# Dividing attended rows instead of probabilities, and two changes to when side work waits, in a stacked cross-attention kernel

## Chip, cores and metric

The kernel runs on 1 core of one Trainium2 chip. The metric is the device time of one execution in microseconds (us), lower is better; the median of several runs is what is compared. The engines are TensorE (PE; its weight loads are listed as PEld), VectorE (DVE), ScalarE (ACT), GpSimd (POOL) and SyncE (SP), which issues the DMAs.

## What is computed

Four attention blocks are applied to x (32 batches of 56 tokens, 160 features) with a context of 1500 keys of 96 features per batch. The parts that matter here:

```python
x = L0(x, ctx)   # three small attentions over 16 keys each, 8 heads; 0.5, 0.5 and 1.0 as weights
x = L1(x, ctx)   # self-attention over 56 tokens (20 heads), cross-attention over 1500 keys, feed-forward
x = L2(x, ctx)   # cross-attention over 1496 keys (8 heads), plus
                 #   ca_hs1 = _mha(ca_q1, residual, residual); ca_hs2 = _mha(ca_hs1 @ Wq, ca @ Wk_ca, ca @ Wv_ca)
x = L3(x, ctx)   # self-attention over 56 tokens (20 heads of 8), cross-attention over 1500 keys, feed-forward

def _attend(q, k, v, scale):
    probs = softmax(q @ k.T * scale)      # exp(s - max) / sum
    return probs @ v
```

## The kernel before, in words

**Phases and pairs.** L0 and L1 form phase 0, L2 is phase 1, L3 is phase 2. In each phase the 32 batches are worked off as 16 pairs; each batch has 64 slots of the 128 partitions. Of the 16 pairs the first and the last are written out, and the 14 between are one hardware loop (`Fori(1, PAIRS - 1)`), so a phase has 13 back edges on every engine.

**Main work.** For each half b of a pair (b = 0, 1) `main` runs over 12 chunks of 125 keys times the groups of heads (3 groups, of 8, 8 and 4 heads, in phases 0 and 2; 1 group in phase 1). For each, TensorE makes scores (L1099 to L1101, three matmuls), ScalarE takes the exponential twice (L1768, L1770), GpSimd forms the low part p_lo (L1557), and two groups later TensorE makes the outputs (L1114 to L1116). Scores and outputs are one step each: a half-pair has 72 steps in phases 0 and 2 and 24 in phase 1. The first scores wait for `mr_ready`, the row maxima written into q_hi (L1417).

**Side work.** Everything else is generators that yield a number before each piece: `pre` (layer norms and the small attentions of the next pair), `queries`, `split`, `context` (transposing the long context in 3 pieces of 500 keys: TensorE L1024, ScalarE ctxT_hi L1726, VectorE ctxT_lo L1391, GpSimd ctx_lo L1538), `maxima` (row maxima over the keys: per tile of queries 3 matmuls L1041, each reduced by VectorE at L1407 or L1404; at the end mneg L1412, its matmul L1046 and q_hi L1417), `post` (projection and feed-forward), `normalise` (the division of the long attention's output, through DRAM). The table `PARTS` gives each part its length in numbers and a weight. `lane` lays parts one behind the other over the steps of a half-pair and scales them to fill it, and `weave` emits each side piece when its position comes due, in the same order on every engine. The second half (b = 1) carries the second part of the next pair's `pre`, then its `queries`, `context` and `maxima`; its lane ends with the half-pair, so the last thing ahead of the next pair's first scores is that pair's q_hi. The first half carries the other batch's `split`, `context` and `maxima`, and `post` and the beginning of `pre`.

**The banks.** Side work uses the PSUM tensor ps_c, whose banks are taken in turn: 3 in phases 0 and 2, and 2 in phase 1 (`banks`). Piece r of the context lies in bank r modulo that number. The first maxima matmul waits for `ctl_ready`, the count of context pieces whose low part VectorE has formed, to have reached all three; then matmul n writes bank n modulo the number of banks.

**The small attentions.** `softmax` on VectorE: maximum (L1188), subtraction (L1190), then ScalarE's exponential (L1594), the sum (L1194), its reciprocal (L1196), and the multiplication of all probabilities by it (L1203), which signals `p_ready`. TensorE's `probs_T` (L732) waits for that, transposes the probabilities; ScalarE copies them out (L1684 in phase 2), `out_slots` (L741) multiplies them with the values (40 matmuls of 16 columns in phase 2), VectorE copies the attended rows out into oz (L1353 in phase 2; L1307 and L1327 in phase 1), `out_T` (L750) transposes them and `project` (L758, L666) projects them. Phase 0 has two such attentions per pair, phase 1 two (the second over 4 keys per head, `p2`), and phase 2 one (10 tiles of 128 columns).

Of the kernel before, what the change touches and what calls it, by code (L numbers as in the profile page):

```python
# [69 lines left out]
class At:  # L70
# [27 lines left out]
    "s_psum": ((2, 2, 1), 0), "s_max": ((2, 2, 1), 0), "s_sub": ((2, 2, 1), 0), "s_exp": ((2, 2, 1), 0),  # L98
    "s_sum": ((2, 2, 1), 0), "s_rec": ((3, 2, 1), 0), "p_ready": ((2, 2, 1), 0),
    "pt_psum": ((2, 2, 1), 0), "pt_ready": ((2, 2, 1), 0), "o_psum": ((2, 2, 1), 0), "o_ready": ((2, 2, 1), 0),  # L100
# [31 lines left out]
def xattn_stack(nc, a, sel, hmask, hmask32, out):  # L132

    es = ExitStack()
    with es:
# [265 lines left out]

        POST = 16

        def schedule(eng, side, main):
# [43 lines left out]

            def lane(parts, start=0.0):

                slots = 2 * NC * len(groups(HEADS[now["ph"]])) - start
                total = sum(length for _, _, length, _ in parts)
# [20 lines left out]
            def apart(steps):  # L473

                return steps, []
# [20 lines left out]
            def pair(t, first=False, last=False):  # L496
# [10 lines left out]
                else:  # L507
                    weave(main(t, 0, first=first), lane(parts + end), *norm)
                parts, start = [], 0.0
                if not last:  # L510
                    parts = [pre_b] + before(t + 1, 0)
                elif t.ph < 2:
                    parts, start = [part("pre", side.pre, At(t.ph + 1, 0, ahead=True))], POST + 4.0
                weave(main(t, 1, last=last), lane(parts, start), apart(side.normalise(t, 0)))

# [144 lines left out]
        def _(pe):  # L660
# [8 lines left out]
            class side(Idle):  # L669
# [57 lines left out]
                @staticmethod  # L727
                def probs_T(t, n, tiles, bank):

                    pe.wait_ge(*got("p_ready", t, n + 1))  # L730
                    for k in range(tiles):
                        z = tr(side_banks(t)(0, 128, bank, 128 * k, 128), sm[:, 128 * k:128 * k + 128], ident[:, :])  # L732
                    z.then_inc(*sig("pt_psum"))
# [150 lines left out]
                def pre_1(t):  # L884
# [55 lines left out]
                    yield 22  # L940
                    pe.wait_ge(*got("p_ready", t, 2))
                    tr(side_banks(t)(0, 32, 0, 0, 128), p2[:, :], ident[:, :]).then_inc(*sig("pt_psum"))
# [85 lines left out]
                def maxima(t, b):  # L1028

                    tiles, wide = MAX_TILES[t.ph]  # L1030
                    for k in range(tiles):
                        for r in range(NPIECE):
                            n = NPIECE * k + r
                            yield 1 + n
                            if n == 0:
                                pe.wait_ge(*got("ctl_ready", t, NPIECE * (b + 1)))
                                if b:
                                    pe.wait_ge(*got("ql_ready", t, per("ql_ready", t)))
                            if n >= banks(t):
# [94 lines left out]
        def _(dve):  # L1134
            V = nc.vector

            class side(Idle):
# [47 lines left out]
                def softmax(t, n, src, dst, m, s, axes, half=None):  # L1185
# [10 lines left out]
                    V.reciprocal(s, s).then_inc(*sig("s_rec"))  # L1196
                    k = n + 1 if t.ph else 2 * n + 1
                    dve.wait_ge(*got("s_rec", t, k))
                    if half is not None:
# [4 lines left out]
                        .then_inc(*sig("p_ready"))  # L1204
                    yield

                @staticmethod
# [74 lines left out]
                def pre_1(t):  # L1282
# [22 lines left out]
                    yield 13  # L1305
                    dve.wait_ge(*got("o_psum", t, 1))
                    V.tensor_copy(oz[:, :], side_banks(t)(0, 128, 1, 0, D)).then_inc(*sig("o_ready"))  # L1307
                    yield 17
# [16 lines left out]
                    yield 25  # L1325
                    dve.wait_ge(*got("o_psum", t, 2))
                    V.tensor_copy(oz[:, :], side_banks(t)(0, 128, 1, 0, D)).then_inc(*sig("o_ready"))  # L1327
                    yield 29
# [3 lines left out]
                def pre_2(t):  # L1332
# [18 lines left out]
                    yield 14  # L1351
                    dve.wait_ge(*got("o_psum", t, 1))
                    V.tensor_copy(oz[:, :], C(0, 128, 0, 0, D)).then_inc(*sig("o_ready"))  # L1353
                    yield 18
# [464 lines left out]
```

## Time and profile before

| what | us |
|---|---|
| median of 3 runs | 6804.21 (6771.78 to 6814.81) |
| the profiled execution | 6784.65 |
| its span, first to last instruction | 6782.8 |
| busy in the span: TensorE / its weight loads | 5972.3 / 4873.4 |
| busy: ScalarE / GpSimd / VectorE | 3112.4 / 3018.5 / 2860.2 |

Phase 0 lasts to about 2990 us of the span, phase 1 to about 4210 us, phase 2 to the end; both boundaries hold a prologue in which the weights are folded. TensorE's granted clock over the span is 0.914 of full speed. In the rows below, `<-` behind an idle time names what ended it; "issue" is time in which the engine waited for nothing that the profile shows. In a waits row stand the total, the count and the longest. A timeline row begins with start and duration; `xN` means N instructions merged.

### The profile page before, as it was taken

How to read it: one execution, taken by the hardware profiler on the slowest of the kernel's cores; microseconds unless marked ns; L12 is line 12 of the kernel's file. 1: busy time of each engine (PE TensorE's matmuls, PEld its weight loads, DVE VectorE, ACT ScalarE, POOL GpSimd, SP SyncE). 2: the span in 40 equal slices, each digit the busy share in tenths (PEclk: the TensorE clock that was granted, in tenths of full speed). 3: DMA queues.
4: the chain of work that ended last, by engine and by line, in shares of the span. 5: the costliest groups of instructions: out<-in, count | busy, mean ns of one | idle time of the engine just before them, and what ended most of it. 6: DMA issues, size and time to landing. Idle time of an engine off the chain costs nothing.

```text
span 6782.8 us, 106855 instructions
## 1 busy us (share of the span) xinstructions
PE 5972.3 (88%) x34384; PEld 4873.4 (72%) x34384; DVE 2860.2 (42%) x5026; ACT 3112.4 (46%) x7280; POOL 3018.5 (45%) x2992
## 2 busy tenths in 40 slices
PE   7999998989989999989898988988888888888888
PEld 5777777777777777766666665777777777777776
DVE  1444444444444444424545443544444444444442
ACT  1444444444444444534444442544454444444444
POOL 0344444444444444434545441544444444444545
PEclk8899999999999999979999896999998989989988
DMA  2000000000000000000101011000000000000000
GB/s 50 12 13 14 14 14 14 14 14 14 14 14 14 12 14 14 18 14 22 29 21 29 21 25 24 17 14 14 14 14 14 14 14 17 14 14 14 17 15 9
DMA packets 84450, 114.90 MB, mean 17 GB/s; under 512 B 42814, under 2 KB 64682, under 8 KB 83978
## 3 DMA queue, kind: packets, MB, share of 16 engines
q1 hardware_dynamic: 83978, 108.56, 5.8%
q8 instruction: 302, 4.95, 0.3%
q14 instruction: 170, 1.39, 0.1%
HBM read 104.06 MB, written 4.46 MB: 16 GB/s over the span
## 4 chain that ended last, share of the span: by engine, by line
PE 67%; issue 10%; DVE 9%; ACT 7%; POOL 4%; DMA 2%; ACTq 0%; DVEq 0%; POOLq 0%; SPq 0%
PE ps_c L666 13%; PE ps_c L1041 7%; PE ps_u L1114 6%; PE ps_s L1099 6%; PE ps_s L1100 5%; PE ps_s L1101 5%; PE ps_u L1115 5%; PE ps_u L1116 5%; POOL p_lo L1557 3%; PE ps_c L1060 3%; ACT p_hi L1770 2%; PE ps_c L732 1%; PE ps_c L1081 1%; PE ps_c L844 1%; PE ps_c L741 1%
## 5 line engine op out<-in xcount | busy, mean ns | idle before, releaser
L1557 POOL TENSOR_TENSOR p_lo<-p,p_hi 125x448 fp32r<-125x448 f32 (+2 forms) x2688 | 2708.2, 1018 | 2957.6 <-ACT p_hi L1770 2755.9
L1768 ACT ACTIVATE p<-ps_s 125x448 f32<-125x448 f32 (+2 forms) x2688 | 1323.3, 492 | 2502.2 <-PE ps_s L1101 2286.4
L1407 DVE TENSOR_REDUCE mpiece<-ps_c 125x1 f32<-125x500 f32 (+1 forms) x1984 | 1287.2, 674 | 339.8 <-PE ps_c L1041 320.6
L1770 ACT ACTIVATE p_hi<-ps_s 125x448 fp32r<-125x448 f32 (+2 forms) x2688 | 1313.7, 489 | 0.0
L1099 PE MATMUL ps_s<-q_hi,ctxT_hi 105*125 105x448 f32 (+3 forms) x2688 | 1029.0, 383 | 181.2 <-issue 86.5
L1114 PE MATMUL ps_u<-p_hi,ctx_hi 125*97 125x448 f32 (+2 forms) x2688 | 1026.8, 382 | 85.3 <-POOL p_lo L1557 78.9
L1041 PE MATMUL ps_c<-ctxT_hi,q_hi 96*125 96x500 f32 (+1 forms) x2112 | 874.9, 425 | 131.9 <-DVE ctxT_lo L1391 87.8
L1100 PE MATMUL ps_s<-q_lo,ctxT_hi 96*125 96x448 f32 (+2 forms) x2688 | 961.5, 358 | 0.0
L1101 PE MATMUL ps_s<-q_hi,ctxT_lo 96*125 96x448 f32 (+2 forms) x2688 | 956.8, 356 | 0.0
L1115 PE MATMUL ps_u<-p_hi,ctx_lo 125*96 125x448 f32 (+2 forms) x2688 | 950.8, 354 | 0.0
L1116 PE MATMUL ps_u<-p_lo,ctx_hi 125*97 125x448 f32 (+2 forms) x2688 | 949.6, 353 | 0.0
L1099 PEld LDWEIGHTS ps_s<-q_hi,ctxT_hi 105*125 105x125 f32 (+2 forms) x2688 | 534.9, 199 | 287.6 <-issue 151.6
L1114 PEld LDWEIGHTS ps_u<-p_hi,ctx_hi 125*97 125x97 f32 (+1 forms) x2688 | 465.5, 173 | 233.6 <-POOL p_lo L1557 137.9
L1041 PEld LDWEIGHTS ps_c<-ctxT_hi,q_hi 96*125 96x125 f32 (+1 forms) x2112 | 403.2, 193 | 276.0 <-DVE mpiece L1407 94.5
L1100 PEld LDWEIGHTS ps_s<-q_lo,ctxT_hi 96*125 96x125 f32 (+1 forms) x2688 | 540.7, 201 | 55.5
L1101 PEld LDWEIGHTS ps_s<-q_hi,ctxT_lo 96*125 96x125 f32 (+1 forms) x2688 | 539.2, 201 | 41.0
L1115 PEld LDWEIGHTS ps_u<-p_hi,ctx_lo 125*96 125x96 f32 (+1 forms) x2688 | 467.3, 174 | 96.1
L1116 PEld LDWEIGHTS ps_u<-p_lo,ctx_hi 125*97 125x97 f32 (+1 forms) x2688 | 464.0, 173 | 90.1
L666 PE MATMUL ps_c<-hT,w_m 80*96 80x128 f32 x3072 | 376.0, 283 | 20.6 <-ACT hT L1587 19.4
L666 PEld LDWEIGHTS ps_c<-hT,w_m 80*96 80x96 f32 x3072 | 361.9, 170 | 35.5 <-issue 29.8
L1538 POOL TENSOR_TENSOR ctx_lo<-ctx_raw,ctx_hi 125x1152 fp32r<-125x1152 f32 x96 | 238.9, 2488 | 317.3 <-DVE ctx_hi L1385 317.3
L1365 DVE TENSOR_TENSOR q_lo<-ps_c,q_hi 96x224 fp32r<-96x224 f32 x192 | 74.3, 387 | 444.1 <-ACT q_hi L1705 444.1
(234 smaller groups left out, 6097.4 us busy)
## 6 DMA issues: line engine op xcount, KB each, us to landing
ctx_raw<-in_ctx SPq DMA_DIRECT2D x96, 562.5 KB
pT<-recs SPq DMA_DIRECT2D x32, 420.0 KB, 3.3
w_area<-recs SPq DMA_DIRECT2D x32, 420.0 KB, 3.3
w_area<-recs SPq DMA_DIRECT2D x32, 168.0 KB, 3.5
cs<-in_ctx SPq DMA_DIRECT2D x192, 6.0 KB, 2.7
x_between<-x_out SPq DMA_DIRECT2D x32, 80.0 KB
x_in<-x_between SPq DMA_DIRECT2D x32, 80.0 KB
w_area<-in_L_xattn_wq SPq DMA_DIRECT2D x2, 800.0 KB, 5.7
```

The lines of the kernel that those rows point to most:

```text
L666: z = mm(dst, lhsT(i), rhs(i), start=(first and i == 0), stop=(last and i == 1))
L1041: mm(C(0, wide, n % banks(t), 0, PIECE), q_hi[0:DC, b, wide * k:wide * k + wide], ctxT_hi[0:DC, b, PIECE * r:PIECE * r + PIECE], start=Tru ...
L1099: mm(dst, ctxT_hi[0:rows_, b, k], q_hi[0:rows_, b, q], start=True, stop=False)
L1100: mm(dst, ctxT_hi[0:DC, b, k], q_lo[:, b, q], start=False, stop=False)
L1101: mm(dst, ctxT_lo[:, b, k], q_hi[0:DC, b, q], start=False, stop=True).then_inc(*sig("sc_psum"))
L1114: mm(dst, ctx_hi[0:kp, cb, c, :], p_hi[0:kp, s, 0:w], start=(c == 0), stop=False)
L1115: mm(ps_u[0:DC, g, 0:w], ctx_lo[0:kp, cb, c, :], p_hi[0:kp, s, 0:w], start=False, stop=False)
L1116: mm(dst, ctx_hi[0:kp, cb, c, :], p_lo[0:kp, s, 0:w], start=False, stop=(c == NC - 1)).then_inc(*sig("pv_done"))
L1407: z = V.tensor_reduce(mpiece[0:wide, k, r:r + 1], C(0, wide, n % banks(t), 0, PIECE), AX.X, ALU.max)
L1557: P.tensor_tensor(p_lo[0:kp, k % 3, 0:w], p32[0:kp, k % 2, 0:w], p_hi[0:kp, k % 3, 0:w].bitcast(F32), ALU.subtract).then_inc(*sig("pl_ready"))
L1768: A(p32[0:kp, k % 2, 0:w], ps_s[0:kp, k % 2, 0:w], ACT.Exp, scale=DH[t.ph] ** -0.5)
L1770: A(p_hi[0:kp, k % 3, 0:w], ps_s[0:kp, k % 2, 0:w], ACT.Exp, scale=DH[t.ph] ** -0.5)\
```

## The change

In phases 1 and 2 the small attentions no longer multiply the probabilities by the reciprocal of their sum. TensorE transposes the bare exponentials (it waits for `s_exp`), and VectorE multiplies the attended rows by the reciprocals while it takes them out of PSUM (`weigh`, in place of the copy into oz). Phase 0 keeps its multiplication. The first matmuls of the maxima wait only for the context piece that their own bank held, or that they read. And the side lane of a pair's second half is scaled to end three steps before the half-pair does.

```diff
-    "s_sum": ((2, 2, 1), 0), "s_rec": ((3, 2, 1), 0), "p_ready": ((2, 2, 1), 0),
+    "s_sum": ((2, 2, 1), 0), "s_rec": ((3, 2, 1), 0), "p_ready": ((2, 0, 0), 0),
...
+        TAIL = 3
...
-            def lane(parts, start=0.0):
+            def lane(parts, start=0.0, tail=0):
 
-                slots = 2 * NC * len(groups(HEADS[now["ph"]])) - start
+                slots = 2 * NC * len(groups(HEADS[now["ph"]])) - start - tail
...
-                parts, start = [], 0.0
+                parts, start, tail = [], 0.0, 0
                 if not last:
-                    parts = [pre_b] + before(t + 1, 0)
+                    parts, tail = [pre_b] + before(t + 1, 0), TAIL
                 elif t.ph < 2:
                     parts, start = [part("pre", side.pre, At(t.ph + 1, 0, ahead=True))], POST + 4.0
-                weave(main(t, 1, last=last), lane(parts, start), apart(side.normalise(t, 0)))
+                weave(main(t, 1, last=last), lane(parts, start, tail), apart(side.normalise(t, 0)))
...
-                    pe.wait_ge(*got("p_ready", t, n + 1))
+                    pe.wait_ge(*got("p_ready" if t.ph == 0 else "s_exp", t, n + 1))
...
-                    pe.wait_ge(*got("p_ready", t, 2))
+                    pe.wait_ge(*got("s_exp", t, 2))
                     tr(side_banks(t)(0, 32, 0, 0, 128), p2[:, :], ident[:, :]).then_inc(*sig("pt_psum"))
...
-                            if n == 0:
-                                pe.wait_ge(*got("ctl_ready", t, NPIECE * (b + 1)))
-                                if b:
-                                    pe.wait_ge(*got("ql_ready", t, per("ql_ready", t)))
+                            if n == 0 and b:
+                                pe.wait_ge(*got("ql_ready", t, per("ql_ready", t)))
+                            if n < NPIECE:
+                                last = max(x for x in range(NPIECE) if x % banks(t) == n % banks(t))
+                                pe.wait_ge(*got("ctl_ready", t, NPIECE * b + max(n, last) + 1))
...
                     V.reciprocal(s, s).then_inc(*sig("s_rec"))
-                    k = n + 1 if t.ph else 2 * n + 1
+                    if t.ph:
+                        yield
+                        return
+                    k = 2 * n + 1
...
+                def weigh(t, n, bank):
+
+                    dve.wait_ge(*got("o_psum", t, n + 1))
+                    dve.wait_ge(*got("s_rec", t, n + 1))
+                    each = [128, t.heads, D // t.heads]
+                    V.tensor_tensor(oz[:, :].rearrange("p (h d) -> p h d", h=t.heads),
+                                    side_banks(t)(0, 128, bank, 0, D).rearrange("p (h d) -> p h d", h=t.heads),
+                                    ssum[:, 0:t.heads].unsqueeze(2).broadcast_to(each), ALU.mult).then_inc(*sig("o_ready"))
...
-                    dve.wait_ge(*got("o_psum", t, 1))
-                    V.tensor_copy(oz[:, :], C(0, 128, 0, 0, D)).then_inc(*sig("o_ready"))
+                    side.weigh(t, 0, 0)
```

The last replacement is phase 2's; phase 1's two copies are replaced in the same way, with bank 1.

## Rows read from the trace of the kernel before

**Rows 1.** The page: busy time, share of the span, instructions.

```profile
PE 5972.3 (88%) x34384; PEld 4873.4 (72%) x34384; DVE 2860.2 (42%) x5026; ACT 3112.4 (46%) x7280; POOL 3018.5 (45%) x2992
```

**Rows 2.** TensorE's waits, phase 2 (4210 to 6783 us).

```profile
PE ps_c L732 <- DVE sm L1203: 76.6, 15, 5.1
...
PE ps_s L1099 <- issue: 40.4, 13, 3.6
...
PE ps_c L1041 <- DVE ctxT_lo L1391: 31.9, 32, 2.1
```

**Rows 3.** TensorE's waits, phase 0 (0 to 2990 us).

```profile
PE ps_s L1099 <- issue: 46.1, 13, 3.7
PE ps_c L1041 <- DVE ctxT_lo L1391: 42.9, 32, 2.6
```

**Rows 4.** TensorE's waits, phase 1 (3005 to 4100 us).

```profile
PE ps_s L1099 <- DVE q_hi L1417: 30.3, 32, 1.2
...
PE ps_c L1041 <- DVE mpiece L1407: 12.4, 17, 0.8
```

**Rows 5.** Timeline of a phase-2 pair around the softmax (5111 to 5133 us).

```profile
5111.76 1.14 ACT L1594 ACTIVATE sm<-sm 128x1120 f32<-128x1120 f32 x1 [5.17 <-DVE sm L1190]
...
5114.60 2.13 DVE L1203 TENSOR_TENSOR sm<-sm,ssum 128x1120 f32<-128x1120 f32 x1
...
5116.78 2.39 PE L732 MATMUL ps_c<-ident,sm 128*128 128x128 f32 x10 [5.11 <-DVE sm L1203]
...
5121.19 1.24 ACT L1684 ACTIVATE pT<-ps_c 128x1280 f32<-128x1280 f32 x1
...
5122.49 4.05 PE L741 MATMUL ps_c<-vb_s,pT 128*64 128x16 f32 x40 [1.01 <-ACT pT L1684]
...
5133.02 0.40 PE L758 MATMUL ps_c<-w_s,ones 1*128 1x160 f32 x1 [0.26 <-ACT xT L1687]
```

**Rows 6.** Windows: us, busy per engine (PE, PEld, DVE, ACT, POOL), granted clock, DMA share, GB/s.

```profile
5115.40:5132.50 17.10, 14.71 (x79) 13.21 (x79) 3.02 (x5) 4.36 (x9) 3.07 (x4) 0.50 0.02 5
5443.00:5446.40 3.40, 2.41 (x41) 2.39 (x42) 0.08 (x1) 1.44 (x3) 1.75 (x2) 0.99 0.00 0
5446.40:5450.00 3.60, 3.60 (x12) 2.83 (x12) 0.25 (x1) 0.98 (x2) 0.28 (x1) 0.53 0.02 5
```

**Rows 7.** A group of VectorE's instructions in phase 2: count | busy, mean ns | idle.

```profile
L1166 DVE TENSOR_TENSOR x_mid<-x_mid,ps_c 128x160 f32<-128x160 f32 x15 | 4.8, 322 | 107.3 <-PE ps_c L666 107.3
```

**Rows 8.** Timeline of TensorE in the pair at 5438 us.

```profile
5438.27 2.40 PE L732 MATMUL ps_c<-ident,sm 128*128 128x128 f32 x10 [5.12 <-DVE sm L1203]
...
5443.99 2.30 PE L741 MATMUL ps_c<-vb_s,pT 128*64 128x16 f32 x40 [1.01 <-ACT pT L1684]
...
5452.03 0.40 PE L758 MATMUL ps_c<-w_s,ones 1*128 1x160 f32 x1 [0.69 <-ACT xT L1687]
```

**Rows 9.** Timeline at a first maxima matmul: phase 2 (5030), then phase 0 (1382).

```profile
5030.89 0.49 PE L1041 MATMUL ps_c<-ctxT_hi,q_hi 96*125 96x500 f32 x1 [0.95 <-DVE ctxT_lo L1391]
...
5032.54 0.45 PE L1114 MATMUL ps_u<-p_hi,ctx_hi 125*97 125x448 f32 x1 [0.61 <-POOL p_lo L1557]
...
1382.70 0.49 PE L1041 MATMUL ps_c<-ctxT_hi,q_hi 96*125 96x500 f32 x1 [0.92 <-DVE ctxT_lo L1391]
...
1382.85 1.16 POOL L1557 TENSOR_TENSOR p_lo<-p,p_hi 125x448 fp32r<-125x448 f32 x1 [0.67 <-ACT p_hi L1770]
...
1384.98 0.37 PE L1114 MATMUL ps_u<-p_hi,ctx_hi 125*97 125x448 f32 x1
```

**Rows 10.** Timeline of stage ends in phase 0: a back edge (1403), and outside the loop (2817).

```profile
1403.41 0.38 PE L1046 MATMUL ps_c<-ident,mneg 125*9 125x125 f32 x2
1403.83 1.34 DVE L1417 TENSOR_TENSOR q_hi<-ps_c,ident 9x1125 fp32r<-9x1125 f32 x1 [0.73 <-PE ps_c L1046]
1407.48 0.46 PE L1099 MATMUL ps_s<-q_hi,ctxT_hi 105*125 105x448 f32 x1 [3.69 <-issue]
...
2817.48 0.47 PE L1099 MATMUL ps_s<-q_hi,ctxT_hi 105*125 105x448 f32 x1 [1.43 <-DVE q_hi L1417]
```

More of the change, by code:

```diff
@@ L1205, in softmax @@
                     yield
+                @staticmethod
+                def weigh(t, n, bank):
[5 more added lines that the diff above has]
+                                    ssum[:, 0:t.heads].unsqueeze(2).broadcast_to(each), ALU.mult).then_inc(*sig("o_ready"))
                 @staticmethod
@@ L1305, in pre_1 @@
                     yield 13
-                    dve.wait_ge(*got("o_psum", t, 1))
-                    V.tensor_copy(oz[:, :], side_banks(t)(0, 128, 1, 0, D)).then_inc(*sig("o_ready"))
+                    side.weigh(t, 0, 1)
                     yield 17
@@ L1325, in pre_1 @@
                     yield 25
-                    dve.wait_ge(*got("o_psum", t, 2))
-                    V.tensor_copy(oz[:, :], side_banks(t)(0, 128, 1, 0, D)).then_inc(*sig("o_ready"))
+                    side.weigh(t, 1, 1)
                     yield 29
@@ L1351, in pre_2 @@
                     yield 14
-                    dve.wait_ge(*got("o_psum", t, 1))
-                    V.tensor_copy(oz[:, :], C(0, 128, 0, 0, D)).then_inc(*sig("o_ready"))
+                    side.weigh(t, 0, 0)
                     yield 18
```

## Prediction, made before the changed kernel was timed

> **What bounds the kernel now.** I read the page's busy times first: TensorE is busy 88% of the span, no other engine reaches half [rows 1]. So a microsecond counts if TensorE loses it, and the next views are TensorE's own waits, phase by phase. In phase 2 the reader sees 76.6 us in 15 waits for the multiplication of the probabilities (L1203), 31.9 us in 32 waits for the low part of the transposed context (L1391), and 40.4 us in 13 waits marked "issue" at the first scores of a stage (L1099) [rows 2]. Phase 0 has 42.9 us and 46.1 us of the last two [rows 3]; phase 1 has 30.3 us in 32 waits for q_hi, its row maxima [rows 4]. All three parts of the change aim at these waits.
>
> The timeline of one phase-2 pair shows how the largest comes about: the exponential on ScalarE ends at 5112.90, VectorE's multiplication starts at 5114.60 (its sum and reciprocal lie between), and the ten transposes start at 5116.78, after 5.11 us without work [rows 5]. Behind it the granted clock is 0.50, that is the 1.2 GHz level, for 17.1 us [rows 6]. So the wait has a second price, paid by all the work behind it.
>
> **Part 1, division on the attended rows (phases 1 and 2).** The transposes wait for the exponential instead of the multiplication. In phase 2 they can start some 0.05 us after 5112.90, so at 5112.95: 3.83 us earlier, and 1.3 us of the wait stays. 15 pairs in the loop and at its ends: 57 us; the sixteenth, started under phase 1, is in no row here, and I give it 3 us. The sum and the reciprocal move beside TensorE's transposes and are long done when the attended rows arrive. The new product replaces a copy from the same bank on the same engine; the nearest row is an addition of 128x160 with an operand from PSUM, 322 ns [rows 7], and the copy takes as many elements from there. I put 0. The broadcast operand is not in that row; at worst it costs that time once more, 0.32 us or 5 us in 15 pairs, and it cannot gain, since it still waits for the same product. In phase 1 TensorE hardly waits there; 0.
>
> What is late next: ScalarE's copy of the transposed probabilities, 1.24 us [rows 5]. From the first transpose to the first of the 40 narrow products (L741) it is 5.71 us, 1.01 us of it waiting for that copy [rows 5]. The copy does not get faster with TensorE, so this wait grows.
>
> Clock: in one pair (5438) the clock had come back before the narrow products; they took 2.30 us instead of 4.05 us, a ratio of 1.76, and the stretch from the first transpose to the bias matmul (L758) took 13.76 us instead of 16.24 us [rows 5, 8]. In that pair it fell again right behind the narrow products, to 0.53 on average [rows 6]: 40 products with 16 columns, a wait of 1.01 us ahead of them and no stall of 5 us. So I expect one such fall after the change as well. Estimate for the changed stretch: 4.5 us to the narrow products (4.70 us of work divided by 1.76 is 2.7 us, and ScalarE's exponentials and copy leave a wait of 1.8 us), 2.3 us for them, and 5.7 us from their end to the bias matmul as in the pair at 5438: 12.5 us, 3.7 us less than 16.24. Bounds: 0 if the clock stays low, and 5.4 us if it never falls (15.0 us of work divided by 1.76, plus 2.3 us of waits, is 10.8). I take 3.2 us, since the shorter wait may still pull it down in some pairs: 48 us in 15 pairs.
>
> **Part 2, maxima wait for their own piece.** With three banks (phases 0 and 2) the first maxima matmul waits for the first of three pieces instead of the last; with two banks (phase 1) piece 2 lies in bank 0, so the first one still waits for all, and nothing changes. The waits sum to 42.9 + 31.9 = 75 us, the upper bound. But GpSimd stands behind them: by the order of the code it forms ctx_lo (L1538) just then, and is late with p_lo. At 5030.89 TensorE has waited 0.95 us for the piece, and at 5032.54 it waits another 0.61 us for p_lo [rows 9]. A wait removed ahead of a wait for GpSimd only lengthens that one: gain 0 in phase 2. In phase 0's later half-pair the p_lo that started at 1382.85 ends at 1384.01, and the product that needs it starts at 1384.98 [rows 9]: 0.97 us of room, so the 0.92 us wait can go nearly whole. I take 0.85 us for 16 of phase 0's 32 waits, 14 us; nothing for the other 16, where ctx_lo stands as in phase 2. Lower bound 0.
>
> **Part 3, the lane ends three steps early.** The chain at a stage's end (mneg, its matmul, q_hi) then lies beside three steps of main work. Outside the loop's back edge that wait is 1.43 us in phase 0 (2817.48). At the back edge it is 3.69 us, though q_hi ended at 1403.83 + 1.34 = 1405.17, 2.3 us before the scores start [rows 10]. So something else ends last there: the jump back. I judge that it starts when the last instruction ahead of it has been issued (1403.41), and that the wait for q_hi already lies inside it. Then 13 back edges in each of phases 0 and 2 keep their 3.1 to 3.5 us; only the matmul of the maxima moves away from them. I take 0.4 us for 13 edges in phase 0, 5 us, and 3 us for the edges outside the loop. If the jump only begins after the wait, the gain would be up to 1.43 us for 26 edges, 37 us.
> The Trainium skill has a rule that bears on this (Runtime: NRT & Kernel Launch, "Instruction fetch mechanics"): a taken branch whose target is not in the engine's small instruction buffer forces a fetch before execution goes on. By that rule the back-edge wait stays whatever the lane does, and the sum keeps its 5 us; without it, 37 us. The trace agrees in that the wait outlasts q_hi by 2.3 us there.
> In phase 1 the wait is 30.3 / 32 = 0.95 us at both edges of a pair [rows 4]; the tail covers one of the two, 15 times: 13 us. Price: the lane has 21 of 24 steps there, so VectorE's reductions come 12.5% denser, and TensorE already waits 12.4 us for them (L1407) [rows 4]. I put 8 us, bounds 0 and 25 (that wait twice over). In phases 0 and 2 the squeeze is 3 steps of 72: 0.
>
> **The sum.** 57 + 3 + 48 + 14 + 5 + 3 + 13 - 8 = 135 us. I take 15 us off, since the pair gets shorter and other stretches may fall to the low clock that do not now (about a third of a microsecond per pair): 120 us. The profiled execution took 6784.65 us (span 6782.8), so 6665 us. It lies 20 us under the median of the runs shown (6804), inside their spread; I stay with the profiled one's base.
>
> **Rivals.** (a) The clock stays low (0.20). The stall shrinks, but the transposes and the narrow products hold the clock down and its 48 us do not come; for it: it fell behind the narrow products in the pair at 5438, too; against it: in that pair it had first come back. Gain 60 + 14 + 8 + 5 = 87 us: 6698 us. The Trainium skill speaks for this rival (TensorE: Matmul & The Clock Gate, "Part 4: PE-mode transpose": transposes do not count as TensorE activity the way matmuls do); no row here shows transposes alone pulling the clock down.
> (b) The other waits go whole (0.12): GpSimd is not next and the back edge really waited for q_hi. 60 + 48 + 75 + 37 + 15 - 15 = 220 us: 6565 us. Against it: the 0.61 us at 5032.54 and the 2.3 us behind q_hi.
> (c) The squeezed lane costs what it can (0.13): 25 us in phase 1 and as much in phases 0 and 2 (their reductions wait for TensorE today, so less is likely): 120 - 17 - 25 = 78 us of gain, 6707 us.
> (d) Slower (0.05). The mechanism is the clock in the rest of the pair: stalls at back edges and at the feed-forward part now fall otherwise against the clock's changes, and each may drag a low stretch like the 17.1 us one behind it. Such a stretch costs 17.1 x (1 - 1/1.76) = 7.4 us. It decides from 16 of them on; one in each of the 31 pairs left of phases 0 and 2 would cost 230 us: 6895 us. Against it: nothing in the change lengthens a stall in those places.
> That the transposes keep waiting as long as before (the exponential being late by itself) is excluded by the 3.83 us between it and them.
>
> **How the numbers follow.** Forecast 0.50 at 6665 us, (a) 0.20, (b) 0.12, (c) 0.13, (d) 0.05. The range from 6590 to 6740 holds the forecast, (a) and (c) whole and leaves out (d) and most of (b). About 1% is what a measurement of this kernel can tell from no change, 68 us: the forecast lies beyond it, (a) and (c) close to it. Faster 0.80, same 0.15, slower 0.05.
>
> **What would show it.** In the changed profile the first transpose in phase 2 should wait about 1.3 us for ScalarE's L1594 instead of 5.1 us; the wait of the narrow products for ScalarE's copy should grow from 1.0 to about 1.8 us; the granted clock behind the transposes should be 1.00 with one fall behind the narrow products, and phase 2 should be shorter by about 100 us. The first maxima matmul should hardly wait in phases 0 and 2, with the waits of L1114 for p_lo grown in phase 2. At the back edges of phases 0 and 2 more than 2.7 us should remain; in phase 1 the wait for q_hi should halve. If the clock stays at 0.50 behind the transposes, (a) holds; if the back-edge wait falls to 2 us, my reading of the jump is wrong; if phases 0 and 1 are longer than before, (c) or (d).

## The result, and the profile after: 6829 us instead of 6665

The changed kernel takes 6828.88 us (median of 20 runs, 6742.27 to 6892.47) against 6777.74 us of the kernel before (20 runs beside it, 6727.82 to 6814.81). The ratio is 1.0061, 95% interval 1.0036 to 1.0085: 0.6% slower, and 164 us above the forecast. (The ratio counts, of each kernel, the executions within 1.5% of its fastest, 14 of 20 after the change and all 20 before; so it lies below the 1.0075 of the two medians.) The span of the profiled execution is 6825.6 us (before 6782.8), its mean granted clock 0.896 (before 0.914).

The busy times of the page, answering to [rows 1]:

```profile
PE 6130.0 (90%) x34384; PEld 5012.1 (73%) x34384; DVE 2825.0 (41%) x4978; ACT 3119.6 (46%) x7280; POOL 3025.1 (44%) x2992
```

The number of TensorE's instructions is the same, and it is busy 158 us longer: more than the whole difference, while its idle time in the span fell by 115 us (810.5 to 695.6). The same matmuls ran slower. The waits, first phase 2 (4243 us on) of the changed kernel, answering to [rows 2]:

```profile
PE ps_u L1116 <- POOL p_lo L1569: 76.9, 102, 2.0
PE ps_s L1101 <- issue: 42.3, 13, 3.7
...
PE ps_c L725 <- DVE xn L1183: 39.6, 30, 2.5
PE ps_c L667 <- ACT hT L1599: 23.0, 15, 1.5
...
PE ps_c L1043 <- DVE ctxT_lo L1403: 4.0, 8, 0.9
```

The two waits that parts 1 and 2 aimed at are gone: none for the multiplied probabilities (76.6 us before), 4.0 us for ctxT_lo (31.9 before; the row for p_lo took on 23.2 us in exchange, from 53.7). The last but one row is new: 15 waits of 1.53 us for hT. Phase 0 of the changed kernel, answering to [rows 3]:

```profile
PE ps_s L1101 <- issue: 42.1, 13, 3.6
PE ps_c L725 <- DVE xn L1183: 36.6, 32, 2.4
PE ps_u L1116 <- POOL p_lo L1569: 30.6, 43, 1.5
...
PE ps_c L667 <- ACT hT L1599: 21.4, 32, 1.0
...
PE ps_c L1043 <- DVE ctxT_lo L1403: 8.6, 15, 1.2
```

Here the wait for xn is the one to look at: 36.6 us in 32 waits, where before it was 8.0 us in 17. (The wait for hT, 21.4 us, was 34.7 us in 32 before.) And phase 1 of the changed kernel (3005 to 4100 us, as before; it begins some 50 us later here, and over 3060 to 4140 us the first row is 17.6 us in 17), answering to [rows 4]:

```profile
PE ps_s L1101 <- DVE q_hi L1429: 16.8, 16, 1.2
PE ps_c L1043 <- DVE mpiece L1419: 16.1, 32, 0.8
```

The waits alone do not explain the time: the new ones sum to about 50 us, the removed ones to more. The group of instructions that does is the queries' matmuls (hT by w_m), here of the kernel before and then of the changed kernel (count, then busy us and mean ns of one):

```profile
L666 PE MATMUL ps_c<-hT,w_m 80*96 80x128 f32 x3072 | 376.0, 283 | 20.6 <-ACT hT L1587 19.4 <-ACT w_n L1579 1.2
```

```profile
L667 PE MATMUL ps_c<-hT,w_m 80*96 80x128 f32 x3072 | 577.8, 372 | 30.3 <-ACT hT L1599 29.1 <-ACT w_n L1591 1.2
```

201.8 us more for the same 3072 matmuls. They come in blocks of 80 (one block in each pair of phases 0 and 2; the other 512 belong to phase 1), and a block is either at a mean of 273 ns or at 389 to 422 ns, with nothing between. Counted from the trace, leaving out the first block of each phase: none of 30 is slow before; after the change 12 of 15 are slow in phase 0 and 13 of 15 in phase 2. Windows of the changed kernel (us, busy of PE, PEld, DVE, ACT and POOL, granted clock, DMA share, GB/s): a fast block of phase 0, a slow one, the stretch around a softmax in phase 2, and a slow block of phase 2:

```profile
2472.00:2496.00 24.00, 23.21 (x162) 21.23 (x163) 13.70 (x24) 11.84 (x31) 10.07 (x9) 1.00 0.10 30
2644.00:2669.00 25.00, 24.25 (x110) 23.07 (x109) 4.63 (x9) 6.67 (x19) 3.95 (x4) 0.52 0.00 1
5136.00:5153.00 17.00, 16.12 (x117) 12.09 (x117) 7.47 (x9) 8.36 (x18) 7.91 (x8) 1.00 0.09 27
5159.00:5184.00 25.00, 25.00 (x121) 23.14 (x120) 4.61 (x10) 7.35 (x21) 5.11 (x5) 0.59 0.00 1
```

At the softmax the clock is now full, as forecast; the one fall that was forecast behind the narrow products does not come in this pair. But a new stretch at 1.2 GHz stands behind it, over the queries: what part 1 gave in this pair at 5136 to 5153 us is spent again from 5159 us on.

The timeline shows what stands ahead of such a stretch. First phase 0 of the changed kernel:

```profile
2639.66 0.17 DVE L1181 BATCH_NORM_AGGREGATE mv<-stats 128x2 f32<-128x6 f32 x1
...
2640.62 1.14 POOL L1569 TENSOR_TENSOR p_lo<-p,p_hi 125x448 fp32r<-125x448 f32 x1 [3.48 <-ACT p_hi L1782]
...
2641.72 0.19 POOL L1515 TENSOR_TENSOR ve<-mv,eps 128x1 f32<-128x1 f32 x1
...
2643.32 0.42 PE L725 MATMUL ps_c<-ident,xn 128*80 128x128 f32 x2 [1.91 <-DVE xn L1183]
...
2644.72 1.57 PE L667 MATMUL ps_c<-hT,w_m 80*96 80x128 f32 x6 [0.24 <-ACT hT L1599]
```

The mean and variance (mv) are there at 2639.83, yet GpSimd forms the root's argument only at 2641.72: a long p_lo stands ahead of it in GpSimd's queue, and that waited for ScalarE until 2640.62. TensorE waits 1.91 us at the norm's transposes. In the kernel before the same three instructions stand in this order:

```profile
1364.48 0.19 POOL L1503 TENSOR_TENSOR ve<-mv,eps 128x1 f32<-128x1 f32 x1 [2.46 <-DVE mv L1179]
...
1365.27 0.66 POOL L1557 TENSOR_TENSOR p_lo<-p,p_hi 125x224 fp32r<-125x224 f32 x1
...
1366.09 0.41 PE L724 MATMUL ps_c<-ident,xn 128*80 128x128 f32 x2
```

GpSimd idled for mv, went on with it at once, and TensorE did not wait at the transposes. It waited once, for the copy to hT:

```profile
1368.06 1.96 PE L666 MATMUL ps_c<-hT,w_m 80*96 80x128 f32 x16 [1.24 <-ACT hT L1587]
```

So ahead of a block of phase 0 TensorE idled 1.24 us before the change and some 2.2 us after it, in two parts. In phase 2 of the changed kernel it is ScalarE's queue:

```profile
5155.91 0.41 PE L725 MATMUL ps_c<-ident,xn 128*80 128x128 f32 x2 [0.50 <-DVE xn L1183]
...
5156.98 0.54 ACT L1780 ACTIVATE p<-ps_s 125x448 f32<-125x448 f32 x1 [1.18 <-PE ps_s L1103]
...
5157.84 0.80 ACT L1599 ACTIVATE hT<-ps_c,gb 80x128 f32<-80x128 f32 x2
...
5158.79 2.86 PE L667 MATMUL ps_c<-hT,w_m 80*96 80x128 f32 x16 [1.53 <-ACT hT L1599]
```

The copy to hT stands behind an exponential whose scores TensorE issued after the transposes. In the kernel before it stood ahead of it, and the same 15 waits summed to about nothing.

How this comes from a tail: the lane's scale draws every due time forward, the later the piece the more, and by one to one and a half steps at these places (an estimate: 3 of 72 steps, for pieces 28 to 34 steps into the lane). The pieces of TensorE and those of GpSimd and ScalarE have different offsets within a part, so a shift moves one of them across a step's border and leaves the other. Counted in the traces, with the groups numbered through the written program and a loop body once: in phase 0 the projection went from behind the 125th group of scores to behind the 124th, and the root stayed behind the 125th p_lo; in phase 2 the transposes went from 410 to 409, and the copy stayed at 410. The main work that was to hide the norm's chain had become a step shorter.

### The profile page after: what moved, and what is told of

It is laid out like the page before. It is cut to its first block, busy times and chain, and to the rows that moved or that the text cites. A ratio compares the mean times of both kernels' runs of the same rounds, so it can differ in the third digit from the quotient of the medians.

```text
span 6825.6 us, 106957 instructions
## 1 busy us (share of the span) xinstructions
PE 6130.0 (90%) x34384; PEld 5012.1 (73%) x34384; DVE 2825.0 (41%) x4978; ACT 3119.6 (46%) x7280; POOL 3025.1 (44%) x2992
## 4 chain that ended last, share of the span: by engine, by line
PE 67%; issue 10%; DVE 9%; ACT 7%; POOL 5%; DMA 2%; ACTq 0%; POOLq 0%; DVEq 0%; SPq 0%
PE ps_c L667 15%; PE ps_c L1043 6%; PE ps_u L1116 6%; PE ps_s L1101 5%; PE ps_s L1103 5%; PE ps_s L1102 5%; PE ps_u L1117 5%; PE ps_u L1118 5%; POOL p_lo L1569 4%; PE ps_c L1062 3%; ACT p_hi L1782 2%; PE ps_c L1025 1%; PE ps_c L845 1%; DMA w_area<-recs 1%; PE ps_c L871 1%
## 5 line engine op out<-in xcount | busy, mean ns | idle before, releaser
L1419 DVE TENSOR_REDUCE mpiece<-ps_c 125x1 f32<-125x500 f32 (+1 forms) x1984 | 1267.5, 672 | 292.9 <-PE ps_c L1043 272.8
L1043 PE MATMUL ps_c<-ctxT_hi,q_hi 96*125 96x500 f32 (+1 forms) x2112 | 865.0, 421 | 67.3 <-DVE ctxT_lo L1403 34.6
L667 PE MATMUL ps_c<-hT,w_m 80*96 80x128 f32 x3072 | 577.8, 372 | 30.3 <-ACT hT L1599 29.1
L667 PEld LDWEIGHTS ps_c<-hT,w_m 80*96 80x96 f32 x3072 | 556.1, 241 | 51.7 <-issue 42.0
```

The lines of the kernel that those rows point to most:

```text
L667: z = mm(dst, lhsT(i), rhs(i), start=(first and i == 0), stop=(last and i == 1))
L1043: mm(C(0, wide, n % banks(t), 0, PIECE), q_hi[0:DC, b, wide * k:wide * k + wide], ctxT_hi[0:DC, b, PIECE * r:PIECE * r + PIECE], start=Tru ...
L1419: z = V.tensor_reduce(mpiece[0:wide, k, r:r + 1], C(0, wide, n % banks(t), 0, PIECE), AX.X, ALU.max)
```

## Experiments

Twelve kernels ran, four at a time on one chip, each four with their own runs of the kernel before (medians 6787.84, 6798.68 and 6772.89 us). "The tail" is TAIL. Theory T of the first texts is that the tail stalls the norm; S is that the softmax part and the shorter pair pull the clock down. Each time is the median of 4 to 10 executions.

**1. The changed kernel without its tail.**

```diff
-        TAIL = 3
+        TAIL = 0
```

> The changed kernel with the tail at 0 (parts 1 and 2 of the change stay). Theory T: the squeeze of the second half's lane moves the transposes of the second layer norm (TensorE waits for xn) one step closer to their producer, the wait ahead of the queries grows from 8 to 37 us in phase 0, the granted clock falls there, and the queries then run at the low clock. Under T this kernel is clearly faster than the changed one and than the one before: about 6640 us, ratio 0.98, phase-0 matmuls of the queries at a mean near 283 ns again instead of 372 ns. Rival S: it is the shorter softmax wait and the changed length of a pair that let the clock fall at the queries; then this kernel stays near 6800 us (ratio 1.00) and the queries stay slow in phase 2 at least.

Measured: 6628.46 us, ratio 0.9759 (0.9684 to 0.9834). Two of 30 query blocks are slow. Two rows of its waits in phase 2 hold two terms of the prediction:

```profile
PE ps_c L742 <- ACT pT L1696: 23.4, 15, 1.6
PE ps_c L733 <- ACT sm L1606: 19.3, 15, 1.3
```

1.29 us a wait at the transposes (forecast 1.3), 1.56 us at the narrow products (forecast 1.8). What follows: the rest of the change gains 2.4%, and the tail costs 200 us on top of it. S falls as an account of its own: with parts 1 and 2 and no tail the queries stay fast.

**2. The kernel before with the tail alone** (part 3 of the diff, nothing else).

> The kernel before with only the tail of three steps. T: slower, 6880 us or more (ratio 1.015 or above), with the wait for xn in phase 0 at about 36 us and the queries' matmuls near 370 ns. S: no difference beyond 0.3%, since neither wait nor softmax is changed.

Measured: 6928.38 us, 1.021 times the 6787.84 beside it; there is no interval for it, but its four times (6839 to 6945 us) all lie above the thirteen of the kernel before (6748 to 6819 us). 11 of 15 blocks are slow in phase 0, 3 of 15 in phase 2, although the wait for hT there is the same 23.0 us in 15. So in phase 0 the tail does its harm alone. In phase 2 the same wait mostly did not pull the clock down while the softmax's own stall and its low stretch still stood some 20 us ahead of it. So in phase 2 the tail does most of its harm only with the rest of the change in place, and that much of S is left; the last section has what the traces show of it.

**3. The division part alone** (no tail, maxima as before).

> The kernel before with only the division on the attended rows. T: faster by my terms for this part, 50 to 110 us (ratio 0.984 to 0.993), all of it in phase 2, phase 0 unchanged. S: within 0.3% of before, the low clock in phase 2 moved from behind the softmax to the queries.

Measured: 6687.45 us, ratio 0.9849 (0.9784 to 0.9915), so 102 us of gain (58 to 147).

**4. The maxima part alone.**

> The kernel before with only the maxima waiting for their own piece. T and S: faster by 14 us as predicted up to 40 us (ratio 0.994 to 0.998), since the changed profile shows the wait for ctxT_lo down by 34 us in phase 0 and by 28 us in phase 2 while the wait for p_lo grew by 19 and 23 us.

Measured: 6717.23 us, ratio 0.9922 (0.9889 to 0.9956), 53 us (30 to 75). Its waits in phase 0:

```profile
PE ps_u L1115 <- POOL p_lo L1558: 29.9, 42, 1.5
...
PE ps_c L1042 <- DVE mpiece L1408: 7.4, 19, 0.6
PE ps_c L1042 <- DVE ctxT_lo L1392: 7.1, 13, 1.4
```

and in phase 2:

```profile
PE ps_u L1115 <- POOL p_lo L1558: 82.3, 105, 2.0
...
PE ps_c L1042 <- DVE ctxT_lo L1392: 8.4, 11, 0.9
```

In phase 2 the waits for ctxT_lo lose 23.5 us (31.9 to 8.4) and those for p_lo gain 28.6 (53.7 in the kernel before): the exchange that the prediction named. In phase 0 they lose 35.8 us (42.9 to 7.1), p_lo gains 18.5 (11.4 to 29.9), and the waits of the maxima for a free bank (mpiece) lose 13.2 more (20.6 to 7.4), which the prediction did not have: the whole row of maxima starts earlier. Net 30 us of waits, and the rest of the 53 in work at a higher clock: the 14 inner pairs of phase 0 went from 2459 to 2403 us, at a granted clock of 0.973 where it was 0.961, and those of phase 2 stayed (2248 and 2254 us).

Sorted by the half of the pair, phase 0's waits say more. (Sorted so, by groups of scores and not by the window, the sums differ from the rows above by up to 1 us.) In the second half ctxT_lo loses 14.1 us (16.0 to 1.9) and p_lo gains 0.3. In the first half ctxT_lo loses 21.7 us (27.4 to 5.7) and p_lo takes back 18.1 of them (9.7 to 27.8); what is won there is the wait for a free bank, 14.1 us (20.6 to 6.5).

**5. No tail, and both pieces put late by hand.** This is to bring the loss back without a tail.

```diff
-        TAIL = 3
+        TAIL = 0
...
                         rsqrt(t, 0, mv, ve, rstd, names)
-                        yield 38
+                        yield 38.4
                         rsqrt(t, 1, mv, ve, rstd, names)
...
-                        yield 20
+                        yield 20.4
                         side.norm(t, 1, 0)
```

> No tail at all; two side pieces are put late by hand: GpSimd's reciprocal root of the second norm in phase 0 comes one p_lo later against the projection, and ScalarE's copy to hT in phase 2 one group of exponentials later against the norm's transposes. Theory P (placement: the tail costs because one side piece slips behind a main piece of its own engine, TensorE stalls about 2 us ahead of the queries, and the queries then run at the low clock): the loss comes back without a tail. Waits for xn at L725 in phase 0 of 1.9 us each instead of 0.5, for hT at L667 in phase 2 of 1.5 us each; the mean of the queries' matmuls back from 289 ns to 350 or more; 6780 to 6850 us, 150 to 220 above the run without a tail (6628). Theory D (density: the tail costs because all pieces of the lane come 3/72 closer): 6620 to 6660 us, the queries at 289 ns.

Measured: 6641.75 us, ratio 0.9761 (0.9697 to 0.9826), no slow block. The expectation of P missed. The order did change, but the p_lo that now stood ahead of the root in phase 0 was a short one of 224 columns, which started 0.12 us after mv came and took 0.66 us; the waits for xn were 11.2 us in 32, and those for hT in phase 2 0.6 us each instead of 1.5. The order by itself costs nothing; the length of the wait that it makes has to be looked at. The ninth run does that for phase 0. (The text of its expectation says that the short p_lo had started before the root's data were there; by the trace it started just behind them.) For phase 2 no run made the wait of 1.5 us without a tail.

**6. The changed kernel with its tail, and both pieces put back ahead.**

```diff
                         rsqrt(t, 0, mv, ve, rstd, names)
-                        yield 38
+                        yield 37.8
                         rsqrt(t, 1, mv, ve, rstd, names)
...
-                        yield 20
+                        yield 19.5
                         side.norm(t, 1, 0)
```

> The changed kernel with its tail of 3 steps, and the two pieces put back ahead: the reciprocal root of phase 0 and the copy to hT of phase 2 are each issued one main piece earlier. Theory P: the waits for xn and hT ahead of the queries go (below 0.7 us each), the queries return to about 290 ns, and the time to 6620 to 6660 us, with the tail still there. Theory D: the lane is as dense as in the changed kernel, so it stays at 6800 to 6840 us with the queries at 370 ns.

Measured: 6540.58 us, ratio 0.9618 (0.9556 to 0.968): 288 us below the changed kernel, and 88 below the one without a tail. No slow block. The queries, and the place in phase 0 that waited 1.91 us before:

```profile
L667 PE MATMUL ps_c<-hT,w_m 80*96 80x128 f32 x3072 | 381.0, 283 | 13.6 <-ACT hT L1599 11.7 <-ACT w_n L1591 1.2
```

```profile
2537.31 0.19 POOL L1515 TENSOR_TENSOR ve<-mv,eps 128x1 f32<-128x1 f32 x1 [2.76 <-DVE mv L1181]
...
2539.40 0.41 PE L725 MATMUL ps_c<-ident,xn 128*80 128x128 f32 x2 [0.60 <-DVE xn L1183]
...
2541.14 1.08 PE L667 MATMUL ps_c<-hT,w_m 80*96 80x128 f32 x8 [0.72 <-ACT hT L1599]
```

D falls: the lane is as dense as in the changed kernel. The spans differ by 282 us (6825.6 and 6543.4). Of these the queries' busy time makes 197 (577.8 and 381.0) and the two waits 43 (36.6 less 16.9 for xn in phase 0, 23.0 less nothing for hT in phase 2); the last 40 are other matmuls in the same low stretches and what was not separated. These two waits are not the whole account of idling: the wait for hT in phase 0 and that for p_lo in phase 2 are longer in this run (27.0 and 84.0 us, against 21.4 and 76.9). Taken together, TensorE's busy time is 261 us shorter (6130.0 and 5868.9) and its idle time 21 us. So the low stretches are the price, and the waits only their start.

The gain over the first run was not expected. In phase 2 neither the softmax's transposes nor the narrow products wait for ScalarE any more, nor did they in the changed kernel: the tail carries the exponential ahead there as well, and what is left of part 1's wait goes with it. The 14 inner pairs of phase 2 take 2113 us, against 2182 in the first run.

**7. The tail doubled.**

```diff
-        TAIL = 3
+        TAIL = 6
```

> The tail doubled to 6 steps, nothing else. By the order of the instructions both pieces then fall ahead of the next main piece again, as without a tail. Theory P: 6600 to 6680 us, the queries at about 290 ns, although the lane is squeezed twice as much (phase 1, where it is 6 of 24 steps, may lose up to 20 us). Theory D: twice the squeeze costs more than the changed kernel's: 6850 us or above.

Measured: 6621.92 us, ratio 0.9745 (0.9678 to 0.9813), no slow block. A tail of 3 costs 200 us and one of 6 nothing against none: not the size of the squeeze but on which side of a step each piece falls. Phase 1 did lose, some 70 us over its 14 inner pairs (945 us in the changed kernel, 1015 here, from q_hi to q_hi): there 6 steps are a quarter of the lane, more than the 20 us allowed for. Phase 2 made up for it, with 2099 us against 2182 without a tail, as in the sixth run.

**8. The tail in phase 1 alone.**

```diff
-                    parts, tail = [pre_b] + before(t + 1, 0), TAIL
+                    parts, tail = [pre_b] + before(t + 1, 0), (0, TAIL, 0)[t.ph]
```

> The tail of 3 steps in phase 1 alone, none in phases 0 and 2. Theory P: no slipped piece in phases 0 and 2, so 6610 to 6640 us, as without a tail; phase 1 as in the changed kernel (the wait for q_hi 0.55 us each). If instead phase 1's denser lane is what costs, it stands over 6700 us.

Measured: 6637.51 us, ratio 0.9777 (0.9715 to 0.9839). The same as the first run within the spread; one slow block of 30. Phase 1's denser lane is not what costs.

**9. No tail, the root two pieces late in phase 0.** As the fifth run, with `yield 39.4` in the place of 38.4 and ScalarE's pieces left alone.

> No tail; GpSimd's reciprocal root of the second norm in phase 0 stands two pieces p_lo late (the run before it put it one late, behind a short p_lo of 224 that had started before the root's data were there: a wait of 0.35 us only). Now a long p_lo of 448 stands ahead of it, as in the changed kernel. Theory P as it stands now (the length of TensorE's wait decides, not the order by itself): waits for xn at L725 in phase 0 of 2 to 2.5 us in the loop, the queries of phase 0 at 370 ns or more against 286, phase 0 longer by 60 to 110 us, 6690 to 6750 us in all; phase 2 as without a tail. Theory R (the wait alone costs its own length, and the queries' clock falls for another reason that comes with the tail): 30 us of waits more, queries at 300 ns or less, 6650 to 6670 us.

Measured: 6816.21 us, ratio 1.0084 (1.0056 to 1.0111). All 15 blocks of phase 0 are slow, none of phase 2. Its timeline, and a window over that block:

```profile
2346.98 1.13 POOL L1569 TENSOR_TENSOR p_lo<-p,p_hi 125x448 fp32r<-125x448 f32 x1 [0.96 <-ACT p_hi L1782]
2348.07 0.19 POOL L1515 TENSOR_TENSOR ve<-mv,eps 128x1 f32<-128x1 f32 x1
...
2350.13 0.65 PE L725 MATMUL ps_c<-ident,xn 128*80 128x128 f32 x2 [3.09 <-DVE xn L1183]
```

```profile
2352.00:2380.00 28.00, 26.89 (x122) 25.28 (x122) 7.16 (x13) 7.68 (x21) 5.20 (x4) 0.55 0.05 13
```

This is the direct test: one tiny GpSimd operation (two instructions of 0.19 and 0.55 us), moved back by two p_lo of which the second is a long one, with no tail at all, costs 188 us against the first run (by the medians; by the ratios, 1.0084 less 0.9759, it is 220), in 15 pairs. The waits for xn in phase 0 grew by 46 us (54.3 against 8.0 in the first run), those for hT fell by 11 (23.3 against 34.6); the rest is clock, with TensorE busy for 130 us more (6049.5 and 5919.6). The wait was longer than expected (3.09 us, not 2 to 2.5), and the time is 66 us above the top of what was expected. Theory R falls.

**10 and 11. One repair each.** The changed kernel with only `yield 37.8` (10), and with only `yield 19.5` (11).

> The changed kernel, and only the reciprocal root of phase 0 put back ahead of the long p_lo. Theory P: phase 0 as in the run with both pieces put back (queries at 286 ns there), phase 2 as in the changed kernel (388 ns); 6540 plus phase 2's share of the loss: about 6680 us.

> The changed kernel, and only the copy to hT of phase 2 put back ahead. Theory P: phase 2 as in the run with both pieces put back (queries 273 ns), phase 0 as in the changed kernel (390 ns, waits for xn of about 1.9 us in the loop); about 6680 us. The two single repairs together should make up the 290 us between the changed kernel and the run with both.

Measured: 6672.4 us, ratio 0.9843 (0.9813 to 0.9874), and 6666.53 us, ratio 0.9832 (0.9798 to 0.9866). The queries by phase, first run 10 (phase 0, phase 2), then run 11 (the windows end at 3050 and begin at 4240 us, and cut into run 10's blocks of other phases, so the counts differ):

```profile
L667 PE MATMUL ps_c<-hT,w_m 80*96 80x128 f32 x1344 | 167.5, 286 | 12.3 <-ACT hT L1599 11.7 <-ACT w_n L1591 0.6
...
L667 PE MATMUL ps_c<-hT,w_m 80*96 80x128 f32 x1143 | 237.9, 399 | 21.4 <-ACT hT L1599 21.4
```

```profile
L667 PE MATMUL ps_c<-hT,w_m 80*96 80x128 f32 x1280 | 269.6, 406 | 6.4 <-ACT hT L1599 6.4
...
L667 PE MATMUL ps_c<-hT,w_m 80*96 80x128 f32 x1280 | 159.0, 282 | 1.4 <-ACT w_n L1591 0.6
```

Each repair brings back its own phase and leaves the other slow (14 of 15 blocks in each). By the ratios the changed kernel (1.0061) loses 2.2 and 2.3 points with one repair and 4.4 with both: the two places are independent.

**12. Both repairs, and a tail of 6 steps in phase 2.** As the sixth run, with `(TAIL, TAIL, 2 * TAIL)[t.ph]` in the place of TAIL.

> Both pieces put back as in the run at 6540 us, and a tail of 6 steps in phase 2 (where a step is one of 72), 3 in phases 0 and 1. In the run with 6 everywhere phase 2 was the shortest of all and phase 1 lost 70 us, so phase 2 should gain some 14 us here and phase 1 stay: 6515 to 6545 us.

Measured: 6528.18 us, ratio 0.963 (0.9599 to 0.9661). The lowest time of all, though not the lowest ratio: against the sixth run (0.9618) there is no difference that these runs can tell. Either one is some 3.7% below the kernel before.

All of them in one table; "slow" counts blocks of 80 queries over 380 ns, of 15 in each phase:

| kernel | us | ratio to before | slow, phase 0 | slow, phase 2 |
|---|---|---|---|---|
| before | 6777.74 | 1 | 0 | 0 |
| changed | 6828.88 | 1.0061 | 12 | 13 |
| 1 no tail | 6628.46 | 0.9759 | 2 | 0 |
| 2 tail alone | 6928.38 | (1.021) | 11 | 3 |
| 3 division alone | 6687.45 | 0.9849 | 2 | 0 |
| 4 maxima alone | 6717.23 | 0.9922 | 1 | 0 |
| 5 no tail, root one late, hT late | 6641.75 | 0.9761 | 0 | 0 |
| 6 tail, both put back | 6540.58 | 0.9618 | 0 | 0 |
| 7 tail of 6 | 6621.92 | 0.9745 | 0 | 0 |
| 8 tail in phase 1 | 6637.51 | 0.9777 | 1 | 0 |
| 9 no tail, root two late | 6816.21 | 1.0084 | 15 | 0 |
| 10 tail, root put back | 6672.4 | 0.9843 | 0 | 14 |
| 11 tail, hT put back | 6666.53 | 0.9832 | 14 | 0 |
| 12 as 6, tail 6 in phase 2 | 6528.18 | 0.963 | 0 | 0 |

## Why the prediction was wrong, step by step

**The step that failed** is the last line of part 3: "In phases 0 and 2 the squeeze is 3 steps of 72: 0." It priced the squeeze as density (are the reductions denser?) and not as movement (which piece changes sides with which?). In its place the runs show that the tail moved the projection and the norm's transposes of TensorE over a border of a step, and left the piece of GpSimd (phase 0) and of ScalarE (phase 2) that they wait for. That price is 288 us, from the changed kernel against the sixth run; in phase 2 most of it is paid only with the rest of the change in place (run 2). All else of the change, with the tail, would have come to 6541 us, 124 us better than the forecast.

**Part 1, division: right, and nearly to size.** Forecast 57 + 3 + 48 less the 15 of allowance is 93 us, measured 102 alone (58 to 147). The wait fell to 1.29 us (1.3 forecast), the next late thing was the copy to pT as named, and the ten transposes ran at the full clock, 278 ns each in place of 425. Of the terms, the one of the clock was too large: the stretch from the first transpose to the bias matmul fell from 15.62 to 13.54 us (means of 15 pairs, run 3), 2.1 us and not 3.2, so 31 us and not 48. Its model of 16.24 us was the most frequent pair and not the mean. The product took the place of the copy (323 ns) for nothing, as put (the row answers to [rows 7]):

```profile
L1218 DVE TENSOR_TENSOR oz<-ps_c,ssum 128x160 f32<-128x160 f32 x15 | 4.6, 309 | 0.0
```

**Part 2, maxima: right in phase 2 (0), too small in phase 0.** The term was 14 us for 16 of the 32 waits; measured is 53 us for the part, all of it in phase 0. The 16 waits that were counted gave 14.1 us, to size. The other 16 did go into waits for p_lo, as was assumed (21.7 lost, 18.1 gained). What was put at nothing is a second wait in the same row of matmuls, for a free bank, 14.1 us in the first half, and the clock.

**Part 3 at the back edges: right.** The 13 waits marked "issue" were to keep 3.1 to 3.5 us each; they are 42.1 and 42.3 us in 13 (phases 0 and 2), where they were 46.1 and 40.4 [rows 3, 2]. One of them in phase 0 of the changed kernel, answering to [rows 10]:

```profile
1422.34 0.38 PE L1048 MATMUL ps_c<-ident,mneg 125*9 125x125 f32 x2
...
1422.76 1.34 DVE L1429 TENSOR_TENSOR q_hi<-ps_c,ident 9x1125 fp32r<-9x1125 f32 x1 [1.26 <-PE ps_c L1048]
...
1427.54 0.46 PE L1101 MATMUL ps_s<-q_hi,ctxT_hi 105*125 105x448 f32 x1 [3.15 <-issue]
```

q_hi ended at 1424.10, now with matmuls between it and the jump, and the scores still stand 3.15 us after the last work. The wait outlasts q_hi by 3.4 us where it was 2.3 before: it does not hang on q_hi, and the jump is what is left. The rule of the Trainium skill that the prediction quoted (Runtime: NRT & Kernel Launch, "Instruction fetch mechanics") agrees. In phase 1 the wait for q_hi went from 30.3 to 16.8 us (13 forecast, 13.5 measured), and the reductions cost 3.7 us more (12.4 to 16.1) instead of 8. (Over 3060 to 4140 us it is 17.6, so 12.7 measured.)

**The rivals.** (a), (b) and (c) did not come. Rival (d), at 0.05, had the mechanism: new low stretches in the rest of the pair, deciding from 16 of them on; there are 25. Two things in it were wrong. Its argument against itself, "nothing in the change lengthens a stall in those places", was never looked up for the norm's chain: when a step is moved, everything that it issues counts, on every queue. And a stretch was priced at 7.4 us; 288 us over 25 is 11.5 us, its stall included. The softmax's stretch, which was that price's model, had only 17 us at the low clock, the queries' has 20 to 24.

**The signs that were named** ("if phases 0 and 1 are longer than before, (c) or (d)") pointed the right way: phase 0's 14 inner pairs grew from 2459 to 2520 us, phase 1's fell from 964 to 945, phase 2's stayed (2248 and 2252), from q_hi to q_hi in the traces. Phase 2 was to be 100 us shorter, and is 2113 in the sixth run.

## What to carry to other kernels

When due times of a woven schedule are scaled or shifted, list for every short chain across engines (here projection, statistics, root, xn, transposes, copy, queries) which main piece each link stands behind before and after: the harm comes from the one link that stays while its neighbours cross a border, and it is not proportional to the shift (3 steps cost 200 us, 6 cost nothing). A stall on TensorE is to be priced with the work that stands behind it: ahead of a long row of small matmuls one more microsecond of waiting cost about ten here. And where a change slows a kernel, look first for a group whose count is the same and whose mean duration has grown.

## What the runs showed of the hardware

**The same matmul has two durations, and a block that turns slow stays slow to its end.** One of the queries' matmuls takes 273 ns at the full clock and 420 ns at the 1.2 GHz level; a block of 80 has a mean of 273 ns or of 389 to 422 ns. The slow blocks do not all start slow: in the changed kernel 7 of the 25 are slow from the first matmul, and the other 18 start with 1 to 16 fast ones, the clock falling within the first 2 us. From there on the granted clock stayed at one half to the end of the block and beyond, 20 to 24 us, although TensorE was never idle for long (24.25 of 25 us busy at 0.52 in 2644 to 2669 us); in the fast blocks it stayed at 1.00.

**What the engine did before it fell.** In phase 0, by the waits that ended in the last 2 us ahead of the block or at its start: one wait of 1.2 us, a fall in 6 of 75 blocks (kernel before, runs 1, 3, 4 and 8); 0.60 and 0.72 us, in 0 of 45 (runs 6, 10 and 12); 1.9 and 0.2 to 0.4 us, in 37 of 45 (changed kernel, runs 2 and 11); 3.09 and 0.4 to 0.7 us, in 15 of 15 (run 9). The wait is not all: 8 blocks stayed fast behind the same 1.9 us, the one at 2472 us of the changed kernel among them, and no run here tells why.

In phase 2 the same wait of 1.53 us for hT drew 13 falls of 15 in the changed kernel, 14 in run 10, and 3 in run 2, where the softmax still stalled. These 45 blocks divide by what stood ahead of them. In all 15 that stayed fast, a stretch at the 1.2 GHz level had ended 7.4 to 8.0 us before the block; in all 30 that fell, the last one had ended 12 us or more before it. Windows of one block of each kind: in run 2 the low stretch ahead and the block with what follows, in the changed kernel the 36.7 us at the full clock ahead and the block.

```profile
4723.90:4737.60 13.70, 12.43 (x70) 11.29 (x71) 2.98 (x5) 3.94 (x8) 1.87 (x4) 0.50 0.02 7
...
4745.50:4765.50 20.00, 18.44 (x138) 16.71 (x139) 7.60 (x14) 9.38 (x26) 7.57 (x8) 1.00 0.07 20
...
5122.10:5158.80 36.70, 30.83 (x213) 23.81 (x212) 15.16 (x27) 19.83 (x45) 18.57 (x21) 1.00 0.05 15
5158.80:5178.80 20.00, 20.00 (x92) 19.22 (x92) 1.55 (x4) 3.51 (x13) 1.10 (x2) 0.52 0.00 1
```

In run 2 that stretch is the softmax's, which part 1 takes away. So part 1 may have removed what kept the clock up at the queries of phase 2. This is read from the traces after the fact: no run moved the stretch alone. In phase 0 it divides nothing: there the last low stretch had ended 37 us or more before every one of the 45 blocks behind a wait of 1.9 us, fast or slow.

The Trainium skill (TensorE: Matmul & The Clock Gate, "A second HAM failure mode: psum-queue depth-cycling") says that short idle times between groups of matmuls can make the clock swing between its levels, and that the cost is paid between the bursts. The traces agree on the swing, behind waits of 1.2 to 3.1 us; but here the cost lies in the burst, 20 us and more of it.

**The changed kernel's times scatter more** (6742 to 6892 us, against 6728 to 6815 before), as a kernel's would in which each of 30 blocks may fall or not. Over its 20 runs the time goes with the mean granted clock, 0.911 in the fastest and 0.886 in the slowest. That the number of fallen blocks is the cause was not shown: a trace was kept of one run only.
